# Expert stage of a vision tower: when each token tile's two gathers are issued

## The chip, the cores and the metric

The kernel runs on one core of one Trainium2 chip. The metric is the device time of one execution in microseconds. A measurement of this kernel is the median of a few runs. A TensorE clock of 1.00 in the profile is 2.4 GHz, 0.50 is 1.2 GHz.

## The reference

The reference is one layer of a vision tower on 32 images of 256 channels and 64 x 64 pixels. A tokenizer pools 4 x 4 pixels to one token with an attention over the 16 pixels; a class token is put ahead; a recurrent layer (tanh) follows; then comes a mixture of experts, the part that the change is in:

```python
logits = tokens @ router_w.T
probs = softmax(logits)
rw, re = top_k(probs, 2)
rw = rw / max(rw.sum(-1), 1e-12)
out = tokens
for e in range(8):
    h = gelu(tokens @ w1[e] + b1[e])
    y = h @ w2[e] + b2[e]
    out = out + combine[:, e:e + 1] * y
```

Each of the 8,224 tokens (32 images, 256 tokens and a class token each) has 256 values and goes to two of eight experts. Its result is the token itself plus two rows of expert output, each times its gate.

## The kernel before

**Token tiles and groups.** Tokens lie in 65 tiles of 128 rows (the last, of class tokens, has 32). They are cut into three groups of 31, 23 and 11 token tiles (line 33), so that the experts of an early group can start while later tokens are still being made. Within a group the tokens are sorted by expert: each token's row is sent to two slots of a DRAM array xs by an indirect DMA (scatter, line 415), and the slots are padded so that each tile of 256 slots has one expert. That makes 38, 30 and 18 expert tiles, 86 in all (N).

**The token stage** (the first 1,125 us) makes the tokens; it also scatters the rows of group 0. The change doesn't touch it.

**The expert stage** is a second block in which each engine runs its own loop over step numbers k. An expert tile is loaded by SP seven tiles ahead (load_x), turned by PE with four transposes (line 1530), split into a high and a low half by ACT (1487) and DVE (1604), multiplied by the first weights on PE (twelve matmuls, lines 1550 to 1552), put through the Gelu by ACT (1502), split again by DVE (1599) and multiplied by the second weights on PE (twelve matmuls, 1565 to 1567), whose end raises the semaphore y_ps. DVE evicts the result (y_in, line 1615) one step later, and SP stores it to a DRAM array ys of the group (store_y, 1416). Step k of DVE holds the eviction of tile k-1, the second split of tile k+1 and the first split of tile k+4 (lines 1631 to 1637).

**The way back.** For each token tile t, POOL issues two indirect DMAs (gather, lines 1455 to 1466), which fetch the token's two rows of expert output from ys into one of eight buffers (RF = 8). POOL's queue is: the base rows of the last two token tiles, the scatters of groups 1 and 2 with their loads (34 token tiles), and then all 65 gathers in order. The first gather of a group waits until all expert tiles of the group are stored (1459 to 1461); any gather from the ninth token tile on waits for the final sum that frees its buffer (1462 and 1463). The final sum is two instructions of DVE (1623 and 1628), which wait for both gathers and for the token's own row (hb, loaded by SP, 1422); SP then stores the result (1427).

**The plan of the final sums** is written out ahead (lines 1382 to 1386). A running number, ready, advances by 0.82 steps per token tile, and starts 3.5 steps behind the group's last expert tile; the sum of token tile t stands in step int(ready) + 1 of DVE's loop. SP loads the token's row four steps ahead of it and stores the result three steps behind it. Token tiles whose step would lie beyond the loop (LATE, line 1392) are summed after it. By this plan token tiles 0 to 30 are summed in steps 42 to 67 and 31 to 48 in steps 72 to 86, and 49 to 64, sixteen, after the loop. POOL's gathers don't follow the plan: they are issued as early as their waits allow.

Of the kernel before, what the change touches and what calls it, by code (L numbers as in the profile page):

```python
# [36 lines left out]
TILES = [(2 * P * n + E * (WIDE - 1)) // WIDE for n in SIZES]  # L37
# [59 lines left out]
def group_of(t):  # L97
    return [g for g in GROUPS if FIRST[g] <= t][-1]
# [18 lines left out]
def vit_tower(nc, xc_in, xp_in, cls_tok, ln_q_w, ln_q_b, wqT, ln_kv_w, ln_kv_w_col, ln_kv_b, wk, wvT, projT, proj_b,  # L117
# [6 lines left out]
    with ctx:  # L124
# [3 lines left out]
        def sem(name):  # L128
            return ctx.enter_context(nc.semaphore(name))
# [118 lines left out]
        s = {n: sem(n) for n in names}  # L248
# [76 lines left out]
        def route_scale(pool, t):  # L325

            pool.wait_ge(s["e_ve"], t + 1)
            pool.tensor_tensor(ers[:, :], eve[:, :], half_neg[:, 0:1], ALU.pow).then_inc(s["e_rs"], 1)

        def route_base(pool, t):  # L330

            pool.wait_ge(s["tok_done"], t + 1)
            pool.tensor_tensor(h2[t % 2][:, :], h2[t % 2][:, :], tok[t % 2][:, :], ALU.add).then_inc(s["base_done"], 1)
# [64 lines left out]
        def load_row(sp, t, xrow=xrow, xrow_in=xrow_in, sent=sent, first=0):  # L398

            i, n = (t - first) % len(xrow), (t - first) // len(xrow)  # L400
            if n > 0:
                sp.wait_ge(sent[i], 32 * n)
            row_ready(sp, t)
            sp.dma_start(xrow[i][:, :], rows_dram[t]).then_inc(xrow_in[i], 16)

        def scatter(pool, t, xrow=xrow, xrow_in=xrow_in, sent=sent, first=0):

            g = group_of(t)
            i, q = (t - first) % len(xrow), (t - first) // len(xrow)
            n = B if t == UNITS else P  # L410
            pool.wait_ge(s["slots_done"], g + 1)
            pool.wait_ge(clear[g], 16 * ((2 * TILES[g] + 2) // 3))
            pool.wait_ge(xrow_in[i], 16 * (q + 1))
            for k in range(2):
                pool.indirect_dma_start(xs_dram[g], bass.IndirectOffsetOnAxis(ap=slot_u[k][0:n, t:t + 1], axis=0),  # L415
                                        xrow[i][0:n, :], None).then_inc(sent[i], 16)
# [928 lines left out]
        N = TILES_ALL  # L1345
        BEFORE = [sum(TILES[:g]) for g in GROUPS]
# [32 lines left out]
        def rows_of(t):  # L1379
            return B if t == UNITS else P  # L1380

        ready, final_step = [0.0], {}
        for t in range(T_ALL):
            ready.append(max(ready[-1] + 0.82, BEFORE[group_of(t)] + TILES[group_of(t)] + 3.5))
            if ready[-1] < N:
                final_step[t] = int(ready[-1]) + 1

        def finals_at(k, lag):

# [63 lines left out]
        @block2.gpsimd  # L1453
        def _(pool):
            def gather(pool, t):

                g = group_of(t)
                n, q = rows_of(t), t % RF
                if t == FIRST[g]:
                    for i in range(YS):  # L1460
                        pool.wait_ge(y_out[i], 16 * len(range(i, BEFORE[g] + TILES[g], YS)))
                if t >= RF:
                    pool.wait_ge(s["f_done"], t - RF + 1)
                for k, y in enumerate((y1, y2)):
                    pool.indirect_dma_start(y[q][0:n, :], None, ys_dram[g],  # L1465
                                            bass.IndirectOffsetOnAxis(ap=slot_u[k][0:n, t:t + 1], axis=0)).then_inc(ga_in[q], 16)

            for t in (UNITS - 1, UNITS):
                route_scale(pool, t)
                route_base(pool, t)  # L1470
            ring = (xrow2, xrow2_in, sent2, SIZES[0])
            for t in rest[:RX2 - 1]:
                load_row(pool, t, *ring)
            for t in rest:
                scatter(pool, t, *ring)
                if t + RX2 - 1 in rest:
                    load_row(pool, t + RX2 - 1, *ring)
            for t in range(T_ALL):
                gather(pool, t)
# [219 lines left out]
```

## Time and profile before

| | us |
|---|---|
| Median of three runs | 1481.64 (1477.16 to 1483.23) |
| Span of the profiled execution, first to last instruction | 1542.8 |
| The profiled execution's own time | not shown beside its span |
| Token stage, in the profile | about the first 1,125 |
| Expert stage, in the profile | from about 1,125 to the end |
| Mean granted TensorE clock | 0.962 |

The profile is of one execution, and its span is longer than the timed runs. Busy time of an engine doesn't count its waits; "issue" is time in which an engine waited for nothing that the profile shows. Start times are microseconds from the start of the span.

### The profile page before, as it was taken

Reading aid. Unit: us, or ns where it says so; the run is one execution under the profiler, and the core shown is the slowest. Engines: PE = TensorE matmul, PEld = TensorE weight load, DVE = VectorE, ACT = ScalarE, POOL = GpSimd, SP = SyncE. Lnnn points to the kernel's source line nnn. Section 1 sums busy time; section 2 is a strip of 40 time slices with the busy share of each in tenths; the row PEclk is TensorE's granted clock in tenths of the full one; section 3 lists DMA queues with packets and bytes.
Section 4 is the critical chain, followed back from the end, with each engine's and each line's share of the span. In section 5 each row is a group of like instructions: output and inputs, shape, how many; then the busy total and the mean of one; then the engine's idle time right before and its main releaser. Section 6 shows DMA issues by size and latency. Waiting matters only on the chain. (4 is left out here: it accounts for less than half of the span.)

```text
span 1542.8 us, 63164 instructions
## 1 busy us (share of the span) xinstructions
PE 1342.3 (87%) x25681; PEld 1061.8 (69%) x25681; DVE 1067.5 (69%) x2855; ACT 832.4 (54%) x2065; POOL 711.1 (46%) x854
## 2 busy tenths in 40 slices
PE   4899999999999999999999999999959997688670
PEld 3677777777777777777776776677748896467550
DVE  4677777777777777878666666678756764467464
ACT  1455665655655655555555555555647774355340
POOL 2243343444434434343555555553313777552555
PEclk9999999999999999999999999999989998799795
DMA  7998898988998998988888989897245887687677
GB/s 259 407 307 298 293 308 297 305 295 295 310 297 276 314 293 280 294 278 293 303 309 302 300 306 312 296 313 256 71 153 193 272 283 245 186 267 255 207 232 227
DMA packets 186620, 423.78 MB, mean 275 GB/s; under 512 B 23968, under 2 KB 89312, under 8 KB 186208
## 3 DMA queue, kind: packets, MB, share of 16 engines
q1 hardware_dynamic: 170336, 380.27, 73.2%
q0 software_dynamic: 14048, 38.16, 7.8%
q8 instruction: 209, 3.42, 0.9%
q10 hardware_dynamic: 1952, 1.32, 0.3%
q14 instruction: 75, 0.61, 0.1%
HBM read 332.26 MB, written 87.39 MB: 272 GB/s over the span
## 5 line engine op out<-in xcount | busy, mean ns | idle before, releaser
L1146 DVE BATCH_NORM_STATS2 st<-xp 128x6 f32<-128x512 f32 x512 | 339.8, 695 | 16.4 <-DMA xp<-xpix 16.0
L656 POOL TENSOR_TENSOR rs_px<-px_ve,half_neg 128x16 f32<-128x16 f32 x64 | 187.0, 2922 | 179.9 <-DVE px_ve L1151 179.9
L770 ACT ACTIVATE zT<-bank 128x512 f32<-128x512 f32 x256 | 138.7, 597 | 75.3 <-PE bank L983 75.2
L1465 POOL DMA_INDIRECT y<-ys_dram,slot x130 | 126.3, 971 | 112.5 <-DVE fin L1628 47.1
L641 POOL TENSOR_TENSOR q_rs<-q_ve,half_neg 128x1 f32<-128x1 f32 x64 | 35.1, 549 | 289.7 <-DVE q_ve L1163 289.7
L763 ACT ACTIVATE z_s<-bank 128x512 f32<-128x512 f32 x256 | 138.6, 597 | 49.0 <-PE bank L973 49.0
L942 PE MATMUL bank<-xc,u 128*32 128x64 f32 x8192 | 149.4, 220 | 17.6 <-issue 17.0
L942 PEld LDWEIGHTS bank<-xc,u 128*32 128x32 f32 x8192 | 132.1, 110 | 41.3 <-issue 32.2
L893 PE MATMUL bank<-xp,spread 128*32 128x256 f32 x2048 | 140.4, 390 | 19.7 <-DMA xp<-xpix 13.4
L744 ACT ACTIVATE u<-bank 128x512 f32<-128x512 f32 x256 | 132.2, 602 | 41.5 <-PE bank L921 41.4
L983 PE MATMUL bank<-ident,z_s 128*128 128x128 f32 x1024 | 150.3, 279 | 1.9 <-issue 1.0
L415 POOL DMA_INDIRECT xs_dram<-xrow,slot x130 | 131.3, 1010 | 39.4 <-issue 34.8
L973 PE MATMUL bank<-xp,pd 64*32 64x256 f32 x4096 | 129.0, 382 | 3.2 <-ACT u L744 3.2
L1502 ACT ACTIVATE g<-bank,b_s 128x256 f32<-128x256 f32 x172 | 82.5, 480 | 82.5 <-PE bank L1552 41.4
L1615 DVE SCALAR_TENSOR_TENSOR y_s<-bank,b_rep 128x512 f32<-128x512 f32 x86 | 59.3, 690 | 94.3 <-remote 41.5
L983 PEld LDWEIGHTS bank<-ident,z_s 128*128 128x128 f32 x1024 | 111.6, 141 | 14.4 <-issue 1.6
L893 PEld LDWEIGHTS bank<-xp,spread 128*32 128x32 f32 x2048 | 64.9, 111 | 71.6 <-issue 37.2
L1158 DVE BATCH_NORM_STATS2 qst<-rT 128x6 f32<-128x256 f32 x64 | 27.2, 426 | 118.3 <-ACT rT L725 118.3
L1565 PE MATMUL bank<-xp,gh 128*128 x344 | 96.0, 279 | 12.1 <-issue 8.1
L1215 DVE TENSOR_TENSOR h_s<-bank,rc 128x256 f32<-128x256 f32 x64 | 27.2, 425 | 114.0 <-PE bank L1002 114.0
L1550 PE MATMUL bank<-xT,xp 128*128 128x256 f16 x344 | 96.4, 280 | 9.4 <-issue 9.3
L1551 PE MATMUL bank<-xT,xp 128*128 128x256 f16 x344 | 96.6, 281 | 7.9 <-issue 7.9
(195 smaller groups left out, 3398.5 us busy)
## 6 DMA issues: line engine op xcount, KB each, us to landing
xp<-xpix SPq DMA_DIRECT2D x256, 512.0 KB
xc<-xg SPq DMA_DIRECT2D x256, 512.0 KB
xc<-xs_dram SPq DMA_DIRECT2D x86, 256.0 KB
ys_dram<-y_s SPq DMA_DIRECT2D x86, 256.0 KB
xs_dram<-zero SPq DMA_DIRECT2D x57, 384.0 KB
base_dram<-h SPq DMA_DIRECT2D x65, 128.0 KB
rows_dram<-tok SPq DMA_DIRECT2D x65, 128.0 KB
hb<-base_dram SPq DMA_DIRECT2D x65, 128.0 KB
```

The lines of the kernel that those rows point to most:

```text
L415: pool.indirect_dma_start(xs_dram[g], bass.IndirectOffsetOnAxis(ap=slot_u[k][0:n, t:t + 1], axis=0), xrow[i][0:n, :], None).then_inc(sent[ ...
L656: pool.tensor_tensor(rs_px[:, :], px_ve[:, :], half_neg[:, :], ALU.pow).then_inc(s["px_done"], 1)
L744: act.activation(uv[:, k, :, :, :], BIG[k][:, :].rearrange("p (m a t) -> p m a t", m=CC, t=TS), ACT.Copy).then_inc(s["u_done"], 1)
L763: act.activation(z_s[:, r, 2 * half:2 * half + 2, :].rearrange("p a c -> p (a c)"), BIG[2 * r + half][:, :], ACT.Copy).then_inc(s["z_done" ...
L770: act.activation(zT[:, c, :, :].rearrange("p h (a r t) -> p r h a t", r=2, t=TS)[:, r, :, :, :], BIG[f][:, :].rearrange("p (a h t) -> p h ...
L893: last = mm(FB[32 * k:32 * k + 32, 0:C], spread[:, 24 - 8 * q:56 - 8 * q], xp[u.x][:, 4 * k + q, :], start=(q == 0), stop=(q == 3))
L942: last = mm(SB[32 * k:32 * k + 32, (2 * n + r) * SUB:(2 * n + r + 1) * SUB], u_s[u.two][:, c, g, :, :].rearrange("p h t -> p (h t)"), xc[u ...
L973: last = mm(BIG[2 * r + half][32 * k:32 * k + 32, n * C:(n + 1) * C], pd[64 * r:64 * r + 64, g, :, :].rearrange("p h t -> p (h t)"), xp[v. ...
L983: last = pe.transpose(BIG[f][:, n * P:(n + 1) * P], z_s[:, r, n, c * P:(c + 1) * P], ident[:, :])
L1146: dve.bn_stats(st[:, j, :], xp[u.x][:, 2 * j:2 * j + 2, :].rearrange("p i c -> p c i")).then_inc(s["st_done"], 1)
L1465: pool.indirect_dma_start(y[q][0:n, :], None, ys_dram[g], bass.IndirectOffsetOnAxis(ap=slot_u[k][0:n, t:t + 1], axis=0)).then_inc(ga_in[q] ...
L1551: mm(o, wh, xl, start=False, stop=False)
```

## The change

The plan is replaced. A token tile t gets a gather step, one more than that of the tile before it, and at the earliest one step behind the last expert tile of its group. POOL's gathers of tile t now also wait until that many expert tiles have had their second layer (y_ps), if the number is below 86. The final sum stands two steps after the gather step, if that lies in the loop. So token tiles 0 to 44 are summed one per step, in steps 41 to 85, and 45 to 64, twenty, after the loop. Token tiles 0 to 46 have the new wait; from 47 on the gather step is 86 or more, and there is none.

```diff
-        ready, final_step = [0.0], {}
+        gather_step, final_step = {}, {}
         for t in range(T_ALL):
-            ready.append(max(ready[-1] + 0.82, BEFORE[group_of(t)] + TILES[group_of(t)] + 3.5))
-            if ready[-1] < N:
-                final_step[t] = int(ready[-1]) + 1
+            k = max(gather_step.get(t - 1, 0) + 1, BEFORE[group_of(t)] + TILES[group_of(t)] + 1)
+            gather_step[t] = k
+            if k + 2 < N:
+                final_step[t] = k + 2
...
                 if t >= RF:
                     pool.wait_ge(s["f_done"], t - RF + 1)
+                if gather_step[t] < N:
+                    pool.wait_ge(s["y_ps"], gather_step[t])
```

## Rows read from the trace of the kernel before

**Rows 1.** Windows: engines' busy us (and instructions), granted clock, DMA share, GB/s.

```profile
core 0: us, PE busy (x) PEld busy (x) DVE busy (x) ACT busy (x) POOL busy (x), PEclk, DMA share, GB/s
200.00:250.00 50.00, 47.73 (x1135) 37.70 (x1124) 37.63 (x109) 29.99 (x76) 20.17 (x26) 1.00 0.90 301
1250.00:1260.00 10.00, 10.00 (x94) 9.12 (x92) 6.20 (x10) 6.79 (x17) 6.88 (x9) 1.00 0.85 271
1300.00:1310.00 10.00, 2.62 (x9) 0.81 (x8) 0.97 (x2) 1.57 (x4) 7.56 (x9) 0.62 0.33 98
1440.00:1450.00 10.00, 1.86 (x5) 0.62 (x6) 0.69 (x1) 0.60 (x1) 7.27 (x8) 0.50 0.46 147
1490.00:1500.00 10.00, 6.85 (x36) 4.32 (x36) 4.85 (x10) 3.14 (x8) 4.76 (x6) 0.68 0.59 185
```

**Rows 2.** Timeline of PE from 1297: start, us, engine, line, operation, idle before.

```profile
1298.16 0.28 PE L1550 MATMUL bank<-xT,xp 128*128 128x256 f16 x1
1299.57 0.27 PE L1551 MATMUL bank<-xT,xp 128*128 128x256 f16 x1 [1.13 <-issue]
...
1312.89 0.37 PE L1567 MATMUL bank<-xp,gl 128*128 x1 [1.50 <-issue]
1314.30 0.37 PE L1530 MATMUL bank<-ident,xc 128*128 128x128 f32 x1 [1.03 <-issue]
...
1321.99 0.37 PE L1530 MATMUL bank<-ident,xc 128*128 128x128 f32 x1 [2.43 <-issue]
1325.49 0.37 PE L1550 MATMUL bank<-xT,xp 128*128 128x256 f16 x1 [3.13 <-issue]
...
1330.43 0.60 PE L1530 MATMUL bank<-ident,xc 128*128 128x128 f32 x4
...
1333.49 0.60 PE L1530 MATMUL bank<-ident,xc 128*128 128x128 f32 x4
```

**Rows 3.** Timeline of POOL from 1297, and its longest wait for stores.

```profile
1298.71 0.87 POOL L415 DMA_INDIRECT xs_dram<-xrow,slot  x1 [0.30 <-issue]
1299.88 1.00 POOL L1465 DMA_INDIRECT y<-ys_dram,slot  x1 [0.30 <-issue]
...
1321.19 0.94 POOL L1465 DMA_INDIRECT y<-ys_dram,slot  x1 [0.30 <-issue]
1328.75 0.94 POOL L1465 DMA_INDIRECT y<-ys_dram,slot  x1 [6.62 <-DVE fin L1628]
...
POOL y L1465 <- DMA ys_dram<-y_s: 32.6, 2, 28.1
```

**Rows 4.** The span, and the chain of waits: start, us, what.

```profile
span 1542.8 us, 63164 instructions
...
by line: issue 4.5%; PE bank L1530 2.5%; PE bank L1565 2.4%; PE bank L1552 2.3%; PE bank L1550 2.3%; PE bank L1567 2.3%; PE bank L1551 2.3%; PE bank L1566 2.3%; POOL y L1465 1.3%; another core or an unknown queue 0.5%; DVE gl L1599 0.4%; DV
...
1434.86 0.54 issue
...
1451.28 1.00 issue
```

**Rows 5.** Timeline of DVE from 1290: evictions, final sums, idle before.

```profile
1293.73 0.69 DVE L1615 SCALAR_TENSOR_TENSOR y_s<-bank,b_rep 128x512 f32<-128x512 f32 x1 [0.93 <-issue]
1303.98 0.48 DVE L1623 SCALAR_TENSOR_TENSOR mid<-y,gate,hb 128x256 f32<-128x256 f32 x1 [7.45 <-DMA y<-ys_dram,slot]
1304.50 0.48 DVE L1628 SCALAR_TENSOR_TENSOR fin<-y,gate,mid 128x256 f32<-128x256 f32 x1
...
1328.83 0.69 DVE L1615 SCALAR_TENSOR_TENSOR y_s<-bank,b_rep 128x512 f32<-128x512 f32 x1 [0.34 <-issue]
1329.43 0.68 DVE L1599 TENSOR_TENSOR gl<-g,gh 128x512 f16<-128x512 f32 x1
1330.03 0.68 DVE L1604 TENSOR_TENSOR xT<-bank,xT 128x512 f16<-128x512 f32 x1
1330.63 0.47 DVE L1623 SCALAR_TENSOR_TENSOR mid<-y,gate,hb 128x256 f32<-128x256 f32 x1
...
1331.54 0.48 DVE L1623 SCALAR_TENSOR_TENSOR mid<-y,gate,hb 128x256 f32<-128x256 f32 x1
...
1332.89 0.69 DVE L1615 SCALAR_TENSOR_TENSOR y_s<-bank,b_rep 128x512 f32<-128x512 f32 x1 [0.34 <-issue]
```

**Rows 6.** The chain of waits at the end: start, us, what.

```profile
1507.23 0.70 DVE y_s L1615
1507.95 2.03 DMA ys_dram<-y_s
...
1510.48 0.94 POOL y L1465
...
1537.48 1.97 DMA y<-ys_dram,slot
```

## The prediction

> **What bounds the kernel now.** I read the page's span and the chain of waits first, then windows through the expert stage, and then POOL, DVE and PE in order of time around the places where PE stops. The token stage fills the first 1,125 us; the change does not touch it. In the expert stage PE runs one expert tile each 3.06 us while nothing disturbs it (four transposes at 1330.43, the next four at 1333.49), busy 10.00 of 10.00 us at a granted clock of 1.00 [rows 1, 2]; a clock of 1.00 is the 2.4 GHz level and 0.50 the 1.2 GHz level. It does not stay so. From 1298 to 1325, 27 us, PE trickles: nine matmuls in ten us, then one per 1.4 to 3.5 us, at a clock that falls to 0.50, and the idle time carries the name "issue": PE waits for nothing that the profile shows [rows 1, 2]. The same comes from 1435 to 1452, 17 us [rows 1, 4], and shorter at some other places (6.85 of 10 us busy at 0.68 near 1495). The reader should see two things. Each time POOL has been issuing indirect DMAs back to back for some 4 to 5 us: from 1299.88 it issues 18 gathers at a pitch of 1.25 us without a wait, and the nineteenth waits for a final sum [rows 3]; PE recovers some 4 us after the last of the 18. And DMA is not full in those stretches (0.33 to 0.46 of the 16 engines), so it isn't bandwidth [rows 1].
>
> "Issue" is 4.5% of the chain, 69 us [rows 4]. The median of the timed runs is 1481.64 us, and the profiled execution's span alone is 1542.8 us [rows 4], 61 us more, with what lies around it not shown. In the token stage PE is busy 95% at a clock of 1.00 [rows 1], so little can be missing there. So I take it that most of the trickle belongs to the recorded execution and not to the timed ones. The test is to lay out the expert stage without the trickle and see whether it ends at the median.
>
> **The stage without the trickle.** Step k is the loop turn in which DVE evicts expert tile k-1 (line 1615), makes two halves (1599, 1604) and adds the token tiles due. A step with two token tiles takes 4.06 us (1328.83 to 1332.89), one token tile is 0.91 of that (1330.63 to 1331.54), so a step with one takes 3.15 [rows 5]. Both are over PE's 3.06: DVE sets the pace wherever final sums run. POOL sends off the rows of groups 1 and 2 until 1299.88; the first gather can't start sooner, in either kernel. The first final sum ends at 1304.98 [rows 3, 5]. Before, that is step 42. The plan of the old code puts the other 30 token tiles of group 0 on steps 43 to 67, five of these with two: 20 x 3.15 + 5 x 4.06 = 83.3, so tile 67, the last of group 1, is evicted at 1388.6. From an eviction to the first gather of its group are 3.25 us (1507.23 to 1510.48) [rows 5, 6], so POOL starts group 1 at 1391.9 and needs 23 x 2.51 us (a pair of gathers) to 1449.6. Tile 85 is evicted by then: four steps without a sum at PE's 3.06, then steps 72 to 85 with 17 sums (11 x 3.15 + 3 x 4.06 = 46.8), less 0.6 us in each of the last four, which have no line 1604 any more: 1445.2, and 3.25 later, at 1448.5, its rows can be read. POOL, not PE, carries this kernel's end. From the first gather of group 2 to the end of the span are 32.3 us in the trace (22 gathers, landing, the last sum, the store; 1510.48 to 1542.8) [rows 4, 6]: 1449.6 + 32.3 = 1481.9, against a median of 1481.64. The stage without the trickle ends where the timed runs do, and this is the base of the sum.
>
> **The change, part by part.**
> 1. The first final sum moves from step 42 to 41 (the plan gives t = 0 the gather step 39). POOL is still scattering then, so DVE stands one step earlier in the same wait, which was 7.45 us [rows 5] and becomes some 10.5. Behind it on DVE stand the eviction of the next tile and its halves, so PE loses that step too: 3 us at the start.
> 2. One token tile per step instead of 1.22. Steps 42 to 85 carry 44 sums, one each: step 85 begins 43 x 3.15 = 135.5 after 1305.3, at 1440.8, less 3 x 0.6 for the missing line 1604: 1439. The old plan, with 49 sums in the loop, begins it at 1443. Gain at tile 84 some 4 us.
> 3. The wait for a second layer. The first tiles find it already met (at 1299.88 tile 41 is evicted, so 42 layers are done and the waits for 39 to 42 pass); after some 12 tiles POOL has caught up, 2.51 against 3.15, and is held to one pair per step. Queued behind the waiting POOL instruction are only later gathers. DVE asks two steps, 6.3 us, after the release; a pair takes 2.5 to issue and 2 to land (1.97) [rows 6], so the sums don't wait: no cost in the middle.
> 4. The end. Token tile 46's gathers wait for 85 second layers, that is for tile 84; tiles 47 to 53 have no wait of their own but stand behind it in POOL's queue, as do all of group 2's. Before, POOL was through with all of group 1 at 1449.6. Now it may begin eight pairs at 1436 to 1439 (PE can be a step ahead of DVE's eviction), 8 x 2.51 = 20.1, and reaches group 2 at 1456 to 1459. That is 6.5 to 9.5 us later, and the 32.3 us follow as before. Twenty token tiles are now summed behind the loop instead of sixteen; at 0.91 us each against 2.51 of gathers, that is hidden behind POOL, and so are their loads of the kept rows on SP, which is idle then.
> 5. Forty-seven more waits on POOL (tiles 0 to 46). No row has the price of a wait that is met; it lies between nothing and one issue slot, the 0.30 us that precede every gather that waits for nothing [rows 3]. Only the last of them, tile 46's, lies on the way to the end: at most 0.3 us, taken as nothing, since the scatter and the gather that follow a met wait have the same slot as those without one [rows 3].
>
> Sum: +6.5 by the lower end, as point 4 holds the gain of point 2 already: 1481.6 + 6.5 = **1488 us**. I take the lower end because DVE's evictions there wait for nothing of PE's (0.34 us of issue before the one at 1332.89 [rows 5]): the second layer is done before DVE comes to it.
>
> A rule speaks on the base. The Trainium skill's page "Runtime: NRT & Kernel Launch", section "The ~15µs preamble/postamble breakdown", has a gap between profile and reported time that is the same for all kernels, about 6.2 us. By it the stalls would be in the timed runs as well, and the time that of the faster rival below. The trace disagrees: 61 us. The page "NOTIFIC — the notification-queue block", section "Overflow: three behaviours, one of which stalls the engine", says that the recorder's internal pipeline holds an engine back rather than lose a record; no run here shows it.
>
> **The rivals.**
> *The tail at full price, slower.* Place: POOL behind tile 84. If POOL had slack before (group 1 gathered well before tile 85), the eight pairs cost all they overlap with nothing: 20.1 less the 6 us between tile 84's second layer and the first gather of group 2, +14, or 1496 us. It decides as soon as tile 84 comes less than about 7 us earlier against POOL's old end. For it: in the recorded run POOL indeed sat 32.6 us in two waits for evicted tiles [rows 3]. Against it: that run was slowed in PE alone. Chance 25%.
>
> *The trickle is real, faster.* If the timed runs have it (the 61 us would be elsewhere), pacing removes much: group 0's burst shrinks from 18 gathers to the 8 that are already released, 10 x 1.25 = 12.5 us; group 1's burst, 17 us of trickle, is released pair by pair, some 15 us; of the smaller stalls, 69 - 27 - 17 = 25 us in all, none to all go. With the +14 of the tail: -13 to -38, or 1443 to 1468, and with a third of the smaller ones 1460 us. For it: each stall follows a burst. Against it: the sum above. Chance 25%.
>
> *The wait never binds.* POOL stays behind PE's count all along, and tile 46 comes late for other reasons: 1481.6 us. It needs a pair to take over 3.15 us; the rows show 2.51. Chance 7%.
>
> **How the numbers follow.** A measurement here can tell about 0.5%, 7.4 us. The forecast has 43%; +6.5 with its bounds 0 to +10 lies inside for 36 of these and beyond for 7. Slower: 7 + 25 = 32%. Within: 36 + 7 = 43%. Faster: 25%. The range reaches from 1454, within the faster rival's bounds, to 1497, the tail at full price and a us of waits. The forecast's own range is 1481 to 1492.
>
> **What would show it.** In the changed kernel's profile: the first gather again near 1300 and a DVE wait before it near 10 us; steps with one sum each; PE's "issue" shorter at group 0 and gone at the start of group 1, so that the recorded span may shrink by 15 us or more while the timed runs do not follow; the last token tiles of group 1 gathered behind tile 84, some 38 gathers in one row at the end instead of 22. I am wrong if the timed runs gain as the recorded one does (then the trickle is real), or if gathers in the middle make DVE wait.

## The result and the profile after

The changed kernel takes 1486.49 us (median of 20 runs, 1476.75 to 1490.61) against 1477.06 us before (20 runs, 1463.92 to 1489.39). The ratio is 1.0057 with a 95% interval of 1.0039 to 1.0076: 8.4 us slower (5.8 to 11.2). The recorded execution of the changed kernel took 1487.61 us with a span of 1485.9 us; so 1.7 us lie around a span (1.6 to 1.8 in all twelve later records).

The record of before that stands ahead of the prediction, with its span of 1542.8 us, is no fair partner: none of the timed executions of that kernel lies near it. The comparison below uses a later record of the same kernel (`before_again`, span 1472.1 us). The head of the changed kernel's page, the line of cores of the kernel before, and then the windows around the first gathers, of the changed kernel and of the kernel before; the columns of the windows are those of [rows 1].

```profile
span 1485.9 us, 63203 instructions
```

```profile
core 0: 1472.1 us, clock 0.971
```

```profile
1280.00:1290.00 10.00, 7.21 (x67) 6.31 (x64) 1.73 (x4) 4.76 (x11) 7.61 (x8) 1.00 0.61 188
1290.00:1300.00 10.00, 7.57 (x44) 6.00 (x45) 8.51 (x16) 3.60 (x9) 7.77 (x8) 0.66 0.74 232
1300.00:1310.00 10.00, 10.00 (x94) 9.09 (x93) 8.16 (x16) 7.00 (x17) 7.36 (x8) 1.00 0.95 317
```

```profile
1280.00:1290.00 10.00, 7.27 (x54) 6.01 (x52) 6.60 (x12) 3.88 (x10) 7.87 (x8) 0.83 0.66 205
1290.00:1300.00 10.00, 7.61 (x57) 6.29 (x56) 6.86 (x13) 4.12 (x10) 7.63 (x8) 0.83 0.75 249
1300.00:1310.00 10.00, 9.57 (x87) 8.25 (x86) 8.68 (x17) 7.05 (x17) 7.79 (x8) 1.00 0.98 309
```

POOL issues without a break in both (7.6 to 7.9 of 10 us busy), as in [rows 1], and PE does not trickle: 44 (changed) and 54 (before) matmuls in ten us where it has least, not 9. What is left there is DVE's wait for the first gather, which takes PE with it; the granted clock is 0.66 in one window of the changed kernel and 0.83 in two of the kernel before (each a mean over two levels, 1.2 and 2.4 GHz).

The end of the work decides the time. POOL's timeline of the kernel before: the last gather of group 0, the wait for the stores of group 1, the first gather of group 2; and then the end of its chain of waits.

```profile
1356.43 0.95 POOL L1465 DMA_INDIRECT y<-ys_dram,slot  x1 [0.30 <-issue]
1379.00 0.94 POOL L1465 DMA_INDIRECT y<-ys_dram,slot  x1 [21.62 <-DMA ys_dram<-y_s]
...
1438.90 0.95 POOL L1465 DMA_INDIRECT y<-ys_dram,slot  x1 [0.31 <-issue]
1440.15 1.06 POOL L1465 DMA_INDIRECT y<-ys_dram,slot  x1 [0.30 <-issue]
```

```profile
1466.85 2.20 DMA y<-ys_dram,slot
1469.07 0.48 DVE mid L1623
1469.58 0.47 DVE fin L1628
```

From 1379.00 on POOL issues 68 gathers with no gap but its issue slot: 23 token tiles of group 1 to 1440.15, then the eleven of group 2. Tile 85 was evicted at 1431.67, so its rows did not hold POOL. This is one unbroken run, and it starts when tile 67 is stored.

The same engine in the changed kernel: token tiles 45 and 46 each wait for a second layer (line 1570 is the old line 1567), and what follows stands behind them. The end of its chain of waits is below.

```profile
1429.50 0.95 POOL L1468 DMA_INDIRECT y<-ys_dram,slot  x1 [1.15 <-PE bank L1570]
1430.75 0.94 POOL L1468 DMA_INDIRECT y<-ys_dram,slot  x1 [0.30 <-issue]
1432.58 1.29 POOL L1468 DMA_INDIRECT y<-ys_dram,slot  x1 [0.89 <-PE bank L1570]
1434.18 0.94 POOL L1468 DMA_INDIRECT y<-ys_dram,slot  x1 [0.30 <-issue]
...
1453.25 0.94 POOL L1468 DMA_INDIRECT y<-ys_dram,slot  x1 [0.30 <-issue]
```

```profile
1480.37 2.46 DMA y<-ys_dram,slot
1482.85 0.48 DVE mid L1626
1483.36 0.47 DVE fin L1631
```

Tile 46 goes at 1432.58. Eight pairs take until 1453.25 (20.7 us), and only then does group 2 begin, 16.8 us after tile 85 was evicted (1436.47). Where POOL waited 21.6 us for stores before, it now waits in small pieces all along, and has the work left over at the end. Tile 46's wait is no longer than the others: 0.89 us, behind a pair that was itself held. Without it alone, nine pairs from 1429.50 at 2.58 us (20.7 / 8) would end at 1452.8 by estimate, hardly sooner. It is the pacing of the last tiles of group 1 together that holds POOL back. The views of waits of the whole run (who waited for whom: us in total, times, longest us), first before, then after:

```profile
POOL y L1465 <- issue: 37.2, 122, 0.3
DVE mid L1623 <- DMA y<-ys_dram,slot: 23.6, 15, 5.8
POOL y L1465 <- DMA ys_dram<-y_s: 21.9, 2, 21.6
```

```profile
POOL y L1468 <- issue: 35.6, 102, 2.3
POOL y L1468 <- PE bank L1570: 29.6, 26, 1.6
DVE mid L1626 <- DMA y<-ys_dram,slot: 29.1, 16, 8.3
```

The token stage differs by some us from one execution to the next (the first gather starts at 1274.75 to 1285.94 us in the twelve later records), so the records are compared from the first gather on. That doesn't make them equal: how far the experts are ahead of POOL differs as well, as expert tile 38 shows, which is evicted before any final sum (first column, us before the first gather). The longer this lead, the longer DVE's first wait for a gather (second column, us). Each other number is a start in POOL's or DVE's timeline, or the span, less the start of that record's first gather:

| Record | Lead of tile 38 | DVE's first wait | Tile 67 evicted | Tile 84 evicted | Gather of token tile 46 | First gather of group 2 | End of span |
|---|---|---|---|---|---|---|---|
| before_again | 12.7 | 5.77 | 98.1 | 152.8 | 142.5 | 163.2 | 195.2 |
| before_third | 15.7 | 8.69 | 96.1 | 150.3 | 139.5 | 159.7 | 191.5 |
| changed kernel | 12.2 | 8.27 | 94.1 | 149.0 | 147.0 | 167.7 | 200.4 |
| no_wait | 13.9 | 10.00 | 94.5 | 149.2 | 137.2 | 161.7 | 194.0 |
| wait_first_group | 13.7 | 9.79 | 93.4 | 151.2 | 138.5 | 164.4 | 197.1 |
| wait_tile46 | 15.4 | 11.43 | 96.0 | 150.8 | 148.9 | 169.7 | 201.6 |
| wait_earlier | 13.6 | 9.72 | 94.3 | 148.9 | 140.8 | 161.8 | 194.0 |
| hold16 | 12.2 | 8.32 | 94.9 | 143.8 | 165.0 | 185.8 | 218.3 |
| early_first | 16.8 | 12.92 | 98.4 | 153.1 | 142.1 | 162.5 | 194.7 |
| late_first | 15.2 | 0.81 | 86.4 | 143.6 | 128.6 | 150.1 | 182.1 |
| later_first | 12.7 | none | 86.2 | 146.1 | 130.3 | 153.0 | 187.4 |
| best | 12.7 | 1.94 | 87.8 | 147.6 | 133.2 | 154.8 | 187.6 |

From the first gather of group 2 to the end it is 31.8 to 34.4 us in every row. What decides is when POOL gets there. The two records of before differ by 3.5 us there, so a difference of that size between two rows says little.

### The profile page after: what moved, and what is told of

It is laid out like the page before. It is cut to its first block and busy times, and to the rows that moved or that the text cites. A ratio compares the mean times of both kernels' runs of the same rounds, so it can differ in the third digit from the quotient of the medians.

```text
span 1485.9 us, 63203 instructions
## 1 busy us (share of the span) xinstructions
PE 1310.9 (88%) x25681; PEld 1053.5 (71%) x25681; DVE 1067.5 (72%) x2855; ACT 836.3 (56%) x2065; POOL 713.8 (48%) x854
## 5 line engine op out<-in xcount | busy, mean ns | idle before, releaser
L1468 POOL DMA_INDIRECT y<-ys_dram,slot x130 | 130.2, 1002 | 65.8 <-issue 35.6
L893 PE MATMUL bank<-xp,spread 128*32 128x256 f32 x2048 | 128.9, 390 | 17.9 <-DMA xp<-xpix 13.0
```

The source lines that it names most:

```text
L893: last = mm(FB[32 * k:32 * k + 32, 0:C], spread[:, 24 - 8 * q:56 - 8 * q], xp[u.x][:, 4 * k + q, :], start=(q == 0), stop=(q == 3))
L1468: pool.indirect_dma_start(y[q][0:n, :], None, ys_dram[g], bass.IndirectOffsetOnAxis(ap=slot_u[k][0:n, t:t + 1], axis=0)).then_inc(ga_in[q] ...
```

## The experiments

Ratios are to the kernel before, on the same chip in the same session, with their 95% intervals.

**The kernel before, once more** (`before_again`), and a third record of it (`before_third`). No edit.

> The kernel before, unchanged. My theory: the trickle of PE belongs to the one recorded execution, so this run ends near the median of before (1464 to 1489 us, ratio 1.00), and its record either shows no trickle and a span near 1475, or shows it again while the timed runs stay where they were. Rival (the trickle is part of this kernel): the time or the span goes to about 1540 us in a good share of the executions.

> The kernel before, recorded once more. My theory: no trickle of PE at the bursts of gathers; span near 1475 us. Rival: it comes again, with a span over 1500 us.

Measured: 1474.86 us (1466.39 to 1483.63, 10 runs), ratio 0.9994 (0.9963 to 1.0024), span 1472.1; and 1474.91 us, span 1473.3. Neither record has a trickle, with the same bursts of gathers, and no timed execution of this kernel in any session took over 1489.4 us. From 1140 us on, PE's idle time named "issue" is 2.0 and 3.2 us in all (longest 0.60), and at most 3.2 in any of the twelve later records; the first record has over 50, in pieces of up to 3.13. The 61 us were of that one recorded execution. That PE trickles because POOL issues back to back is refuted as a rule: these two records have the bursts without it. What set it off in the one record was not found. That execution's own time is not on record either.

**No new wait** (`no_wait`). The plan stays, the wait goes.

```diff
-                if gather_step[t] < N:
+                if False:
                     pool.wait_ge(s["y_ps"], gather_step[t])
```

> The changed kernel without the new wait of the gathers on y_ps; the plan of the sums stays. My theory (the loss is eight pairs of gathers held behind expert tile 84): the pairs up to token tile 52 go out as their buffers come free, only tile 53 is late, and the end comes about 7 us earlier than in the changed kernel: ratio to before 1.000 to 1.003. Rival (the loss comes from the plan, one sum per step and the first at step 41): the time stays at the changed kernel's, ratio near 1.006. Second rival (pacing protects PE): slower than the changed kernel.

Measured: 1477.26 us, ratio 1.0007 (0.9981 to 1.0033). The loss is gone, so it came from the wait and not from the plan. In the table the first gather of group 2 is 6.0 us earlier than in the changed kernel. It lies between those of the two records of before. One wait is left in POOL's last run, for a buffer that comes free late, since more tiles are summed behind the loop; it is 3.00 us long.

```profile
1439.47 0.94 POOL L1468 DMA_INDIRECT y<-ys_dram,slot  x1 [3.00 <-DVE fin L1631]
```

**Which wait** (`wait_first_group`: tiles 0 to 30 alone; `wait_tile46`: one tile alone).

```diff
-                if gather_step[t] < N:
+                if t < SIZES[0]:
```

```diff
-                if gather_step[t] < N:
+                if t == 46:
```

> The changed kernel with the new wait for token tiles 0 to 30 alone. My theory: pacing in the middle costs and gives nothing, so this equals the kernel without any new wait, ratio to before 1.000 to 1.003. Rival (the wait costs wherever it stands): ratio near 1.005, as in the changed kernel.

> The changed kernel with the new wait for token tile 46 alone, on 85 second layers. My theory: this one wait makes the whole loss, so the time is the changed kernel's, ratio to before 1.005 to 1.007, although 46 of the 47 waits are gone. Rival (the loss is spread over the waits): the time is that of the kernel without any of them.

Measured: 1477.10 us, ratio 1.0011 (0.9985 to 1.0037), and 1481.73 us, ratio 1.0050 (1.0019 to 1.0080). Thirty-one waits cost nothing that shows; one wait alone costs about what all 47 do. The two intervals overlap a little, but the twelve times of wait_tile46 average 1483.3 us, against 1476.1 of no_wait and 1478.2 of wait_first_group in the same session. The waits of token tiles 31 to 45 were not run without that of 46; by the estimate above they would cost nearly as much. The one wait stands in POOL's timeline as the only one for PE (line 1570), 9.38 us long:

```profile
1417.55 0.95 POOL L1468 DMA_INDIRECT y<-ys_dram,slot  x1 [0.30 <-issue]
1427.87 1.22 POOL L1468 DMA_INDIRECT y<-ys_dram,slot  x1 [9.38 <-PE bank L1570]
1429.40 0.95 POOL L1468 DMA_INDIRECT y<-ys_dram,slot  x1 [0.30 <-issue]
```

**More and fewer pairs behind tile 84** (`hold16` and `wait_earlier`).

```diff
-            if k + 2 < N:
+            if t < 38:
...
-                    pool.wait_ge(s["y_ps"], gather_step[t])
+                    pool.wait_ge(s["y_ps"], gather_step[t] if t < 38 else 85)
```

```diff
-                    pool.wait_ge(s["y_ps"], gather_step[t])
+                    pool.wait_ge(s["y_ps"], gather_step[t] - (2 if t >= SIZES[0] else 0))
```

> The changed kernel with token tiles 38 to 53 held behind expert tile 84 instead of 46 to 53; tiles 38 to 44 are therefore summed behind the loop. My theory (each pair held there costs its 2.51 us of POOL): eight pairs more, 20 us over the changed kernel, ratio to before near 1.019 (1.016 to 1.021). Rival (a fixed cost of waiting for tile 84): ratio stays near 1.006.

> The changed kernel with the wait of token tiles 31 to 46 two expert tiles earlier; tile 46 is released by 83 second layers. My theory: POOL may begin the last eight pairs 6 us sooner, which is most of the loss; ratio to before 1.000 to 1.003. Rival (any wait on y_ps in the last group costs the same): ratio near 1.006.

Measured: 1496.84 us, ratio 1.0168 (1.0113 to 1.0223), and 1476.89 us, ratio 1.0040 (1.0004 to 1.0075). With sixteen pairs held, POOL stands 23 us and then has 41.5 us of gathers (1421.04 to 1462.50, 2.59 us a pair) before group 2:

```profile
1421.04 0.95 POOL L1468 DMA_INDIRECT y<-ys_dram,slot  x1 [23.08 <-PE bank L1570]
1422.30 0.94 POOL L1468 DMA_INDIRECT y<-ys_dram,slot  x1 [0.30 <-PE bank L1570]
1423.54 0.95 POOL L1468 DMA_INDIRECT y<-ys_dram,slot  x1 [0.30 <-issue]
```

Against the changed kernel that is 1.0168 - 1.0057, 16 us, instead of 20 (four executions). In the records group 2 begins 18.1 us later: eight pairs more are 20.8 (41.5 less 20.7), but POOL is released 2.7 us sooner (144.4 against 147.0 after the first gather), as seven sums fewer stand in the loop (tile 84's eviction comes 5.2 us sooner). The price goes with the number of pairs; a fixed cost of the wait is excluded. The other run is inconclusive in its time: the ratio is over the 1.000 to 1.003 that I expected, and its interval holds both theories' values. Its record ends like that of no_wait, 194.0 us after the first gather, as the theory has it; but it is of one execution, 6.5 us under the run's median.

**The first sum's step** (`early_first`, `late_first`, `later_first`; the kernel before with one number changed: 2.5, 6.5, 9.5).

```diff
-            ready.append(max(ready[-1] + 0.82, BEFORE[group_of(t)] + TILES[group_of(t)] + 3.5))
+            ready.append(max(ready[-1] + 0.82, BEFORE[group_of(t)] + TILES[group_of(t)] + (6.5 if t < SIZES[0] else 3.5)))
```

> The kernel before with one number changed: the first group's sums start one step earlier (2.5 instead of 3.5), so the first stands in step 41, as in the changed kernel. My theory, point 1 of the sum: DVE stands in the wait for the first gather a step longer, 3 us: ratio 1.002 (1.000 to 1.004). Rival (the wait is free, since one sum less stands later): ratio 1.000 or below.

> The kernel before with one number changed: the first group's sums start three steps later (6.5 instead of 3.5), so the first stands in step 45. My theory: the first gather can't be issued before POOL's scatters are through, so the early sum only holds DVE and with it the eviction of expert tile 67, from which POOL's last unbroken run starts. Without that wait the run starts about 6 us sooner: ratio 0.996 (0.993 to 0.998). Rival (the wait is caught up behind the loop): ratio 1.000.

> The kernel before with the first group's sums starting six steps later (9.5 instead of 3.5), the first in step 48. My theory: DVE no longer waits at all and fewer sums stand ahead of tile 67, so it is a little under the kernel that starts three steps later: ratio 0.992 (0.988 to 0.996). Rival (POOL's buffers come free too late and its first run breaks up): ratio 0.996 or above.

Measured: 1477.91 us, ratio 1.0020 (0.9997 to 1.0043); 1463.98 us, ratio 0.9935 (0.9907 to 0.9964); 1466.23 us, ratio 0.9923 (0.9898 to 0.9948). One step earlier costs about the 3 us expected, on the edge of what these runs can tell. Three steps later beats both kernels, by more than the 0.996 I expected, though within its range. The timelines of DVE show why (of late_first, before_again, before_third, the changed kernel and early_first, in this order): the wait for the first gather is 0.81 us where it was 5.77 and 8.69 before, 8.27 in the changed kernel and 12.92 in early_first.

```profile
1283.56 0.69 DVE L1615 SCALAR_TENSOR_TENSOR y_s<-bank,b_rep 128x512 f32<-128x512 f32 x1 [1.17 <-PE bank L1567]
1286.26 0.48 DVE L1623 SCALAR_TENSOR_TENSOR mid<-y,gate,hb 128x256 f32<-128x256 f32 x1 [0.81 <-DMA y<-ys_dram,slot]
```

```profile
1281.08 0.48 DVE L1623 SCALAR_TENSOR_TENSOR mid<-y,gate,hb 128x256 f32<-128x256 f32 x1 [5.77 <-DMA y<-ys_dram,slot]
```

```profile
1285.88 0.48 DVE L1623 SCALAR_TENSOR_TENSOR mid<-y,gate,hb 128x256 f32<-128x256 f32 x1 [8.69 <-DMA y<-ys_dram,slot]
```

```profile
1289.66 0.48 DVE L1626 SCALAR_TENSOR_TENSOR mid<-y,gate,hb 128x256 f32<-128x256 f32 x1 [8.27 <-DMA y<-ys_dram,slot]
```

```profile
1290.03 0.48 DVE L1623 SCALAR_TENSOR_TENSOR mid<-y,gate,hb 128x256 f32<-128x256 f32 x1 [12.92 <-DMA y<-ys_dram,slot]
```

Tile 67 is evicted 86.4 us after the first gather instead of 98.1 and 96.1, and POOL's last run starts that much sooner. Against before_third, whose lead is nearly the same (15.7 and 15.2), the 9.7 us are explained: the wait is 7.9 us shorter, and three sums that now stand behind tile 67 are 2.7 (0.91 each), 10.6 in all, less 0.5 for the shorter lead. Against before_again the wait gives 5.0, the sums 2.7 and the longer lead 2.5, and 1.6 of the 11.8 stay open. Three more steps (9.5) bring nothing further that can be told: tile 67 stays at 86.2.

**Fewer sums ahead of tile 67** (`best`): one sum a step from step 44 in group 0, 0.7 steps apart later.

```diff
-            ready.append(max(ready[-1] + 0.82, BEFORE[group_of(t)] + TILES[group_of(t)] + 3.5))
+            ready.append(max(ready[-1] + (1.0 if t < SIZES[0] else 0.7), BEFORE[group_of(t)] + TILES[group_of(t)] + (5.5 if t < SIZES[0] else 3.5)))
```

> The kernel before with the plan of the sums changed: the first group one sum per step from step 44, the others 0.7 steps apart; no wait on y_ps. My theory: tile 67 is evicted about 8 us earlier than before because fewer sums stand ahead of it, and the buffers of the later tiles are freed in time; ratio 0.994 (0.991 to 0.997). Rival (the sums put off hold POOL through the buffers, f_done): ratio 1.000 or above.

Measured: 1465.55 us, ratio 0.9949 (0.9920 to 0.9979): as expected, and no better than the one number.

## Why the prediction was right, and where it was not

The forecast was 1488 us, 0.43% over the three runs then known; measured are 1486.49 us and 0.57% (0.39% to 0.76%). Size and sign hold, and the mechanism is the one named in point 4. The forecast lay just inside the 0.5% that I took a measurement to tell, and the measured change just outside, with an interval that holds both.

*That the trickle is not in the timed runs* was right, and is now shown: two further records of the same kernel are without it. Its size was read too high: the 69 us of "issue" are no measure of the trickle, since the chain of before_again, which has none, holds 5.7% of it, 84 us; PE's own idle time named so is 56 us in the first record from 1120 on. *The base of the sum*, though, came near the median by errors that cancel in part, and the median itself was of three runs, 4.6 us over that of twenty. I kept the first gather at 1299.88 from the disturbed record; it is at 1276.93 and 1281.82 in the undisturbed ones, 18 to 23 us earlier. And I reckoned tile 67 at 88.7 us behind it (1388.6 - 1299.88), where it stands at 96.1 to 98.1. Behind it, POOL's pairs of group 1 took 2.60 and 2.66 us instead of 2.51, so group 2 began 159.7 to 163.2 us after the first gather where the sum has 149.7. The sum ends 8.6 to 9.8 us over the two undisturbed spans (1481.9 against 1473.3 and 1472.1). The step that failed there is "DVE sets the pace": DVE and PE hand waits to each other. The view of waits between 1282 and 1426 us of before_again:

```profile
DVE y_s L1615 <- PE bank L1567: 15.2, 24, 1.2
PE bank L1565 <- DVE gl L1599: 11.3, 11, 2.7
```

So a step is longer than DVE's work of 3.15 and 4.06: from the first sum to tile 67 they average 3.7 us (1282.44 to 1375.07, 25 steps), not 3.33; 2.8 of these 92.6 us are two more waits for early gathers. An agreement with a median proves less than it seems when the start is taken from a record that one does not trust.

*Point 1*: the first waits of single records can't simply be compared, since they follow the lead: 5.77 and 8.69 us before, 8.27 in the changed kernel. Lead less wait is 6.9 and 7.0 us in the two records of before, and 3.9 in all seven records whose first sum stands in step 41. At equal lead the step earlier costs 3.0 to 3.1 us of waiting. Right; early_first alone shows about 3 us by time.
*Point 2*: tile 84 comes 1.3 to 3.8 us earlier (149.0 against 150.3 and 152.8); I had 4. But four other records with this plan of sums have it at 148.9 to 151.2, which overlaps with before. Records of like lead give both: 3.8 us earlier (changed kernel and before_again) and 0.5 later (wait_tile46 and before_third). A gain of 4 us fits, and so does none.
*Point 3*: POOL caught up after 20 gathers, ten tiles (I had twelve); from then on nearly every pair is held (33 of 37 stand longer than the issue slot), and DVE doesn't wait for it: 8.7 us in all between 1290 and 1430, of which 8.3 is the one at the start. Right; wait_first_group shows the same by time.
*Point 4*: eight pairs took 20.7 us (20.1 forecast), and the end behind them 32.65 (32.3). Against the two records of before, group 2's first gather is 4.5 and 8.0 us later; I had 6.5 to 9.5. My reason for taking the lower end, that evictions wait for nothing of PE's, was wrong (see the 15.2 us above). The release was early all the same: tile 84's second layer ended at 1431.83 (its last matmul is below), 2.7 us ahead of the eviction at 1434.53. That the lower end came out is thus in part luck.

```profile
1431.56 0.27 PE L1570 MATMUL bank<-xp,gl 128*128 x1
```

*Point 5*: no price of a met wait shows. In the changed kernel the gathers of token tile 1, whose wait was met, have the same 0.30 us before them as any; and no_wait and wait_first_group differ by 0.0004, each with an interval of 0.0026 (3.8 us) to either side, for 31 waits of which many were not met at once.

```profile
1288.11 0.95 POOL L1468 DMA_INDIRECT y<-ys_dram,slot  x1 [0.30 <-issue]
```

*The rivals.* The tail at full price needed slack in POOL before; there was none, POOL ran unbroken from 1379.00. The forecast for the recorded span, that it would shrink while the timed runs do not follow, came true (1542.8 to 1485.9 against 1477.06 to 1486.49), but for the plain reason that the first record was unlike the others; so it supports no claim on pacing. "The trickle is real" falls with the records without it, and with a changed kernel that is slower. "The wait never binds" falls with the 26 waits for PE.

The Trainium skill's page "Runtime: NRT & Kernel Launch", section "The ~15µs preamble/postamble breakdown", gives 6.2 us by which a profile's total exceeds the reported time. No such surplus shows here: in the twelve later records the span is 1.6 to 1.8 us shorter than the time of its own execution (1485.9 and 1487.61). A span runs from the first to the last instruction, so it need not be the page's total.

## What to carry to other kernels

Find the engine whose last unbroken run ends the kernel, and what starts that run; here it is POOL's gathers, released by one expert tile. A wait put into that queue costs the whole work queued behind it, less what the engine would have waited anyway: thirty-one early ones cost nothing that shows, because POOL had 21.6 us to wait there anyway, and a single late one cost about as much as all 47. Before pacing an engine to cure a stall, record the kernel a second time: a stall of 27 us in one record was in none of the next twelve.

## What was not expected

PE at one matmul per 1.4 to 3.5 us beside POOL's bursts, in one execution, and never again under the same bursts; its cause stays open. The start of the first sum gave 9.6 us (1 - 0.9935 of 1473.27) for three steps later, where I expected 6: the wait depends on the lead, and sums moved behind tile 67 count too. A DVE stall that looks hidden behind the loop moves the eviction that starts POOL's last run.
